# Issue order of x loads and y stores in the sorted experts' stage: three loads ahead of the loop in place of two

## What is computed

```python
logits = xf @ router_w
topk_logits, topk_idx = jax.lax.top_k(logits, K)        # K = 2
topk_w = jax.nn.softmax(topk_logits, axis=-1)
cw = jnp.zeros((T, E), xf.dtype).at[jnp.arange(T)[:, None], topk_idx].add(topk_w)
out = jnp.zeros_like(xf)
for e in range(E):
    h = xf @ w1[e] * jax.nn.silu(xf @ w_gate[e])         # 128 -> 256
    out = out + cw[:, e:e + 1] * (h @ w2[e])             # 256 -> 128
```

## Time and profile before

| | us |
|---|---|
| median of 3 runs | 2966.3 |
| lowest and highest of them | 2955.6, 2970.61 |
| profiled execution, device time | 2961.36 |
| its span, first to last instruction | 2959.6 |
| TensorE busy | 2325.6 (79% of the span) |
| VectorE busy | 2054.7 (69%) |
| GpSimd busy | 1671.3 (56%) |
| ScalarE busy | 1458.8 (49%) |
| `grouped`, first x load issued to last y store issued | 1986.15 to 2226.2 |

### The profile page before, as it was taken

How to read it: one execution, slowest core, us unless ns; L and a number is a source line. 1 busy time by engine, 2 the same in 40 slices (tenths; PEclk the granted TensorE clock), 3 DMA queues, 4 the chain that set the end, 5 groups by cost and what they waited for, 6 DMA issues and landing times. The chain is left out here.

```text
span 2959.6 us, 61920 instructions
## 1 busy us (share of the span) xinstructions
PE 2325.6 (79%) x20767; PEld 1531.8 (52%) x20767; DVE 2054.7 (69%) x5010; ACT 1458.8 (49%) x2472; POOL 1671.3 (56%) x2078
## 2 busy tenths in 40 slices
PE   0015637887878888879999999958887999999997
PEld 0003314443444444656666666638884666666665
DVE  8988826878887787376665666635664777777775
ACT  3434424655555555344554545436664554545553
POOL 4546630424242433146787888754443888887886
PEclk9997757989999899689999999989998999999998
DMA  2030022232222321301111111132221222222222
GB/s 59 0 133 0 0 81 78 66 109 83 88 92 80 103 68 62 104 9 40 45 50 45 42 50 43 47 89 74 83 81 32 62 59 67 58 64 64 65 56 63
DMA packets 200232, 184.54 MB, mean 62 GB/s; under 512 B 36736, under 2 KB 163777, under 8 KB 200002
## 3 DMA queue, kind: packets, MB, share of 16 engines
q1 hardware_dynamic: 191824, 164.98, 19.1%
q0 software_dynamic: 8192, 16.79, 1.9%
HBM read 105.65 MB, written 69.60 MB: 59 GB/s over the span
## 5 line engine op out<-in xcount | busy, mean ns | idle before, releaser
L1868 DVE CUSTOM_DVE_ANT_0 a_scored<-a_pMax,a_causal 128x128 bf16<-128x128 f32 (+3 forms) x1024 | 450.0, 486 | 375.2 <-PE a_pMax L2086 338.7
L1082 DVE TENSOR_REDUCE a_max<-a_pair_banks 128x2 f32<-128x1024 f32 (+3 forms) x512 | 404.7, 820 | 174.6 <-PE a_pair_banks L649 162.3
L1777 ACT ACTIVATE a_PT<-a_pST 128x1024 f32<-128x1024 f32 (+1 forms) x384 | 339.2, 883 | 367.0 <-PE a_pST L2076 341.0
L1006 ACT ACTIVATE a_PT<-a_pair_banks 128x1024 f32<-128x1024 f32 (+1 forms) x384 | 334.2, 883 | 300.7 <-PE a_pair_banks L649 299.6
L1695 POOL TENSOR_SCALAR_AFFINE_SELECT a_PT<-a_PT 128x256 f32<-128x256 f32 x512 | 207.9, 418 | 247.1 <-ACT a_PT L1777 218.7
L2094 PE MATMUL a_pO<-a_PT,a_V 128*64 128x512 f32 (+3 forms) x2048 | 305.6, 441 | 5.7 <-POOL a_PT L1695 5.7
L1713 POOL TENSOR_TENSOR a_SM<-a_PT 128x768 f32<-128x768 f32 x128 | 234.6, 1833 | 10.7
L1303 PE MATMUL a_pair_banks<-a_QS,a_KS 64*128 64x512 bf16 (+3 forms) x1024 | 144.0, 321 | 99.3 <-DVE a_max L1082 58.1
L2094 PEld LDWEIGHTS a_pO<-a_PT,a_V 128*64 128x64 f32 x2048 | 135.8, 137 | 161.3 <-issue 120.4
L1717 POOL TENSOR_TENSOR a_SM<-a_SM,a_PT 128x512 f32<-128x512 f32 x128 | 213.3, 1667 | 10.7
L2069 PE MATMUL a_pST<-a_q_high,a_k_high 64*128 64x512 f32 (+3 forms) x1024 | 200.0, 387 | 20.8 <-ACT a_PT L1777 17.9
(11 more groups left out here) (337 smaller groups left out, 6428.8 us busy)
## 6 DMA issues: line engine op xcount, KB each, us to landing
a_rden<-inverse_sums_dram SPq DMA_DIRECT2D x128, 256.0 KB
a_KS<-k_parts_dram SPq DMA_DIRECT2D x64, 224.0 KB
a_QS<-q_parts_dram SPq DMA_DIRECT2D x64, 192.0 KB
m_x<-x_sorted_dram SPq DMA_DIRECT2D x71, 128.0 KB, 2.3
y_sorted_dram<-m_y SPq DMA_DIRECT2D x71, 128.0 KB, 1.8
x_sorted_dram<-ffn_zeros SPq DMA_DIRECT2D x17, 512.0 KB, 5.1
q_parts_dram<-a_parts SPq DMA_DIRECT2D x16, 384.0 KB
k_parts_dram<-a_parts SPq DMA_DIRECT2D x16, 384.0 KB
```

Of the source, the lines that this page charges most:

```text
L1006: a.activation(PT[p][:, :, at:at + w], score_bank[k][:, :, 0:w], ACT.Exp, scale=SCALE).then_inc(exped.sem, 1)
L1082: last = v.tensor_reduce(MX[:, :, p, j], max_bank[m][:, :, at:at + (j + 1) * P], AX.X, ALU.max, negate=True)
L1777: a.activation(PT[s.q % 2][:, :, k * TOK:k * TOK + w], pST[:, :, 0:w], ACT.Exp, scale=SCALE).then_inc(exped.sem, 1)
L1868: last = v.tensor_tensor_reduce(scored[:, cc, at:at + w], pMax[:, cc, at:at + w], causal[:, TOK - w:], -1.0, 3e38, ALU.add, ALU.min, MX[pa ...
```

## The change

A constant AHEAD = 3 stands in for the 2 that was written out in the SP list. Ahead of its loop SP issues three loads in place of two, and in step i of the loop `load(i + 3)` in place of `load(i + 2)`, before `store(i - 3)` as it was. No other list changes, no buffer is added, and the waits inside `load` and `store` are the same.

```diff
-    DEEP, WDEEP, LAG = 3, 4, 2
+    DEEP, WDEEP, LAG, AHEAD = 3, 4, 2, 3
...
-            load(0)
-            load(1)
+            for i in range(AHEAD):
+                load(i)
             for i in range(NTL + 3):
-                if some(i + 2):
-                    load(i + 2)
+                if some(i + AHEAD):
+                    load(i + AHEAD)
                 if some(i - 3):
                     store(i - 3)
```

## The result

The changed kernel takes 2925.34 us (median of 4 runs, 2920.41 to 2932.85) against 2961.02 of the kernel before (4 runs, 2955.6 to 2970.61). The two medians lie 35.7 us apart, a quotient of 0.988; the ratio on record is 0.9863, 95% interval 0.9841 to 0.9886. Measured once more later, with six runs of it against eleven of before, the ratio was 0.9856 (0.9826 to 0.9886). So the change makes the kernel 1.2 to 1.4% faster.

The account below looks back on a forecast made before the run. PE was held by x loads queued behind stores on SP: 65 steps at 2.60 us give 169.0 against 208.36 us, less 0.5 for slow loads and rounding, so 38.5 off 2966.3 us: 2927.8 us, range 2915 to 2944.

Parts of the forecast that it names:

- What bounded the stage: In `grouped`, PE waits for x loads held on SP behind an unrelated store: 40.4 us in 65 steps of 3.21 us.
- The two moved distances: On SP, a load issued 1.38 us after `turn_y` lands 2.3 us later; need moves to two steps on, 5.2 us.
- the 1.7 us of room: Time claimed between an x load's landing and the `turn_x` that needs it, after the change: 1.7 us, so no wait.
- The slow loads: x loads of up to 4.1 us in `grouped` would still cost 0 to 3 us in all; 0.5 us taken.
- about ten: Number of the 65 x loads taken as slow, 4.1 us at worst, judged by waits of 1.4 us and more.
- The step: One pipeline step of `grouped` without load waits: 2.60 us taken, 2.66 us as upper bound.
- What is late next: After the load waits go, PE and a chain on DVE and ACT limit the step together, at 2.58 us each.
- the ring: Dependent chain `rest_h`, `rest_x`, `make_h` on DVE, `high` on ACT, next `rest_h`: claimed 2.58 us once round.
- The rival on the ring: The DVE and ACT chain takes over at 2.68 to 2.75 us a step, 29.6 us saved, 2936.7 us; chance 14%.
- The sum: Saving over 65 steps of `grouped`: 39.4 us, less 0.5 for slow loads and rounding, 38.5 us.
- The order of the list: Rival: SP's order is not what holds the loads, they wait for `turn_x`; no effect, 2966 us; chance 6%.
- The clock: Rival: TensorE's clock falls to 1.2 GHz in the denser stage; at half the steps 2982 us; chance 2%.

Follow-up runs that it names:

- the second: The changed kernel, unchanged, profiled once more on one chip beside the kernel before: 168.56 us for the 65 steps, against 207.88.
- the added transfer: A scratch transfer of 128 KB issued ahead of each load: 2937.77 us in the changed kernel, 2942.95 us in the kernel before.
- the shorter step: The changed kernel without two layer-2 matmuls per tile and without weight copies from the fifth tile on: 2875.79 us, 2.390 us a step.

## Why the prediction was right

**What bounded the stage.** Right. The store in front of each load was the hold, shown by moving the stores to another queue. The kernel before has a row that shows it and that the prediction doesn't use: SP's waits at the stores, from the view of the earlier trace rows:

```profile
SPq L2266 <- ACT m_y L2320: 163.8, 71, 7.2
```

SP stood at the stores for most of the stage, and at the loads hardly at all. One sum on the way is off: the 3.6 us in (2.6 + 3.6) / 2 = 3.1 run from `turn_y` to `turn_x` and hold a whole short step, so they are no step. The pair of the earlier trace rows gives (2.58 + 3.37) / 2 = 2.98 us, and slow loads made up 0.23 us of the average step of 3.21, twice what was said. The forecast doesn't use this sum.

**The two moved distances.** Right: 1.38 us from `turn_y` to the load in both kernels, and a landing of 2.3 us in both. The need came one step later, with the 1.7 us of room, and the wait went to 0, not just below 3 us.

**The slow loads.** I took 0.5 us for them, with 3 as the bound. They cost 0. In the first profile the longest landing of the middle of the stage was 3.2 us, not 4.1; in the second it was 3.9, and the 65 steps still took 168.56 us. The "about ten" were also not all loads of 4.1 us: those with waits of 1.4 us and more took 2.8 to 4.1. That the room is finite was right, as the added transfer and the shorter step showed.

**The step.** 2.60 us forecast, 2.593 measured. 65 x 2.593 = 168.6 us, against 169.0 forecast.

**What is late next.** Half wrong. PE and the ring were said to be the limit together. PE alone is. The step that failed is the reading of "no visible idle time" in the ring, 2.58 us once round, as a second limit of 2.58 us: one of its parts, `rest_h`, was held until 0.54 us after a copy that PE's layer 2 lets go, and got shorter when it mattered. The rival on the ring had said that it would. The time did not depend on it, since PE's step was as long.

**The sum.** 38.5 us forecast; the stage gave 39.8 and 39.3, the ratio 0.9863 of 2961.02 is 40.6. The medians themselves lie 35.7 us apart, and 44.7 in the later measurement. The forecast of 2927.8 us stood on the median of 2966.3 known then; the measured 2925.34 is 2.5 us under it and inside the range. So close a hit is in part luck, as single runs of either kernel lie 12 to 15 us apart; what the mechanism earned is the 39.8 us of the stage.

**The rivals.** The ring did not take over (its 2.68 to 2.75 us would have needed `rest_h` to be covered by more of the copy; it is 0.94 as before). The order of the list did matter. The clock stayed at 1.00 in the denser stage. It did fall in the kernel with one load ahead, which is the opposite case, with a pause of over 3 us in every step. There the estimate for the level of 1.2 GHz, 1.7 us more in a step, was borne out: from `turn_x` to `turn_y` are 4.18 us, against 2.39 in the changed kernel. The Trainium skill (TensorE: Matmul & The Clock Gate, Part 1) says that activity releases the throttle; both traces agree, with 1.00 at unbroken work and 0.66 at pauses over 3 us, while the 37 pauses of 0.8 to 2.3 us in the kernel before had left it at 1.00.

## What to carry to other kernels

On a queue that is worked off in order, a load inherits the wait of whatever stands in front of it, here a store that waits for the end of the pipeline. Measure from the event that frees the queue to the landing, divide by the length of a step, and place the load so many steps ahead; more brings nothing, and when the steps get shorter the count has to be done again. Count how far ahead a load really goes out, from its issue to the instruction that needs it, and not by the number in the loop. A ring of dependent instructions without idle time is a limit only if none of its parts would shrink under pressure: cut one part and look whether the step follows.

## What the runs showed of the hardware

37 pauses of TensorE of 0.8 to 2.3 us in 65 steps left the granted clock at 1.00; pauses of 3.4 us in every step brought it to 0.66, to which more than a third of what the stage lost is put down. A subtraction of two SBUF tiles on DVE (128x512) took 0.69 us alone, and ended 0.54 us after the end of a GpSimd copy under which it had begun, whether the two overlapped by 0.2 or by 0.5 us; the multiplication with one input in PSUM kept its 0.68 us. An issue of a transfer of 128 KB from ScalarE, one per step of 2.59 us, cost nothing that shows, with ACT busy for 126 of 168.56 us. And doubling the loads, to 150 GB/s, left their median landing at 2.3 us, with single loads of up to 4.0 us as in the kernel before.
